# Whole numbers instead of a rounding operation in a piecewise-linear GELU

## The chip, the cores and the metric

The kernel runs on one core of a Trainium2 chip. The metric is the time of one execution on the device, in microseconds (us), smaller is better. Three runs of the kernel before gave 961.65, 962.42 and 962.64 us.

## The reference

Two transformer layers work on x (8 batches of 256 rows of 256). Each layer is a cross-attention on a context of the same shape and a feed-forward block, both behind a layernorm and with a residual. The feed-forward block of the first layer quantises to FP4. The change touches only the one of the second layer:

```python
def float2fix(x, mantissa_bits):
    s = jnp.float32(2.0 ** mantissa_bits)
    q = jnp.round(x * s) / s
    return x + stop_gradient(q - x)
def pwlin_gelu_basic(x, bits_in, bits_out):
    xq = float2fix(x, bits_in)
    y = jnp.interp(xq, _PWL_X, _PWL_Y)      # 33 knots on [-4, 4], 0.25 apart
    y = jnp.where(xq > 4.0, xq, jnp.where(xq < -4.0, 0.0, y))
    return float2fix(y, bits_out)
h = float2fix(x @ w1 + b1, 8)               # [.., 256] x [256, 1024]
h = float2fix(pwlin_gelu_basic(h, 8, 8), 8)
out = float2fix(h @ w2 + b2, 8)             # [.., 1024] x [1024, 256]
```

So the hidden value is rounded to a whole multiple of 2^-8, the exact GELU is taken at the two knots around it, and a straight line between them gives the result, rounded to 2^-8 again.

## The kernel before, in words

The 2048 rows are worked in four groups of 512. Every engine has its own program, written out by hand in the order in which it is to run; the engines meet only at semaphores. An opening does the first attention of group 0. For each group `fp4_and_layer1` does the FP4 block and the second attention. Between two groups stands a crossing: it does the last feed-forward block of the group that ends, and among it the first attention of the group that begins. There are three crossings, and a closing that does the last block of group 3 alone.

The block that the change touches is worked in eight chunks (m = 0 to 7) of 128 hidden columns by 512 rows. The path of one chunk goes through three engines, in one of four buffers of four slices (`gelu_buf`), with these lines of the profile:

- PE (`last_hidden`) multiplies by w1 into a PSUM bank, four banks in turn; in a crossing it then does the queries of the next group (`layer0_queries`, "ring,wq_s" in rows, tile q0 in banks 0 and 1).
- ACT L522 (`hidden`) evacuates the bank with the bias b1 into slice 0. ACT L527 (`hidden_fixed`) adds FIX = 1.5 x 2^15 to slice 0: fp32 then keeps whole multiples of 2^-8 only, and the last bits of the number are the whole number.
- DVE L838 keeps the bits above the lowest six (the knot, slice 2), DVE L843 keeps the lowest six (the place between the knots, slice 1).
- ACT L531 (`gelu_low`) is the GELU of the knot, ACT L535 (`gelu_high`) that of the knot 0.25 further; both take FIX off again by their bias. L535 waits until L531 is done.
- DVE L834 subtracts the two, L841 multiplies by the place between them, L847 adds the lower one, L849 rounds and writes `yT`. L841, L847 and L849 each wait until the one before is done. Where L849 is done, `y_ready` goes up.
- PE L1137 (`last_out`) multiplies by w2. In a crossing its order is: chunks 0 to 5, then the first scores of the next attention (`layer0_scores`, L1171), then chunks 6 and 7, then a product for the keys of the second attention (`layer1_key`), whose bank ACT empties at L548.

ACT and DVE interleave neighbouring chunks. ACT's order in one step is L522 of chunk m, L531 of m-1, L527 of m, L535 of m-1. DVE's is L834 of m-1, L838 of m, L841 of m-1, L843 of m, L847 and L849 of m-1. In a crossing ACT also puts the two query tiles into its last two steps (L542, two instructions for each, the second tile behind the last L535), and the first scores wait for both. Behind them stand a table load and the exponentials (L593), which wait for DVE's row maxima (L884).

Of the kernel before, what the change touches and what calls it, by code (L numbers as in the profile page):

```python
# [7 lines left out]
I32 = mybir.dt.int32  # L8
ALU = mybir.AluOpType
# [21 lines left out]
MASKED = -1.0e30  # L31
FIX = 1.5 * 2.0 ** 15
STEP = 0.25
KNOT_BITS, LINE_BITS = -64, 63
LINE_BASE = 2.0 ** 17
LINE_BASE_BITS = (127 + 17) << 23
# [175 lines left out]
def xattn_ffn_twice(nc, x, ctxT, mask, wq0, bq0, wk0, bk0, wv0, bv0, wo0, wgate, wup, wdown,  # L212
# [23 lines left out]
    with ExitStack() as ctx:  # L236
        def sb(name, shape, dt=F32):
            return ctx.enter_context(nc.sbuf_tensor(name, shape, dt))

        def sem(name):  # L240
            return ctx.enter_context(nc.semaphore(name))
# [15 lines left out]
        ident_s, ones_by_head = sb("ident_s", [P, P]), sb("ones_by_head", [P, 3, DK0])  # L257
        holder = sb("holder", [P, 1 + UNITS])
        minus_half = sb("minus_half", [P, TILES])
        gelu_bias, two, unused = sb("gelu_bias", [P, 3]), sb("two", [P, 1]), sb("unused", [P, 2])  # L260


        x_s, ctxT_s = sb("x_s", [P, TILES, DM]), sb("ctxT_s", [P, KC, GROUP])
# [57 lines left out]
        max0, inv0, clipped0 = sem("max0"), sem("inv0"), sem("clipped0")  # L321
        bias_ready, exp1, inv1, norm1 = (sem(n) for n in ("bias_ready", "exp1", "inv1", "norm1"))
        silu_ready, hid_ready = sem("silu_ready"), sem("hid_ready")
        g_fixed, g_knot, g_line, g_low, g_high, y_ready = (sem(n) for n in ("g_fixed", "g_knot", "g_line", "g_low", "g_high", "y_ready"))
        o_bias, o_round, out_ready = sem("o_bias"), sem("o_round"), sem("out_ready")

        def is_filled(at, key):
# [87 lines left out]
        @block.gpsimd  # L415
        def _(pool):
            for src, dst in ((bk0, bk0_s), (bq0, bq0_s)):
                for half in range(2):
                    pool.dma_start(dst[64 * half:64 * (half + 1), :], without_padding(src, half), allow_slow_non_contiguous=True).then_inc(keys_loaded, 16)
            pool.memset(minus_half[:], -0.5).then_inc(consts_set, 1)  # L420
            pool.memset(gelu_bias[:, 0:1], -FIX).then_inc(consts_set, 1)
            pool.memset(gelu_bias[:, 1:2], STEP - FIX).then_inc(consts_set, 1)
            pool.memset(v0[:], 0.0).then_inc(consts_set, 1)
            pool.memset(ones_by_head[:, 1, :], 0.0).then_inc(consts_set, 1)
            pool.memset(two[:], 2.0).then_inc(consts_set, 1)

            pool.memset(ones_by_head[:, 0:3:2, :], 1.0).then_inc(consts_set, 1)
            pool.memset(gelu_bias[:, 2:3], FIX).then_inc(consts_set, 1)
            pool.wait_ge(consts_set, 8)

            def ln_power(n):
                for h in range(HALVES):
                    half = slice(2 * h, 2 * h + 2)
                    pool.wait_ge(ln_var, n * HALVES + h + 1)
                    pool.tensor_tensor(rstd[:, half], var_eps[:, half], minus_half[:, half], ALU.pow).then_inc(ln_rstd, 1)  # L435

            def mask_to_bias():

                pool.tensor_scalar(maskbias[:], mask_s[:].bitcast(U8), MASKED, None, ALU.mult).then_inc(bias_ready, 1)

            def normalize_heads(g):

                for i in range(UNITS):
                    pool.wait_ge(inv1, g * UNITS + i + 1)
                    for a in range(2):
                        ins = pool.tensor_tensor(probs1[i % PRING1][:, a, :], probs1[i % PRING1][:, a, :],  # L446
                                                 row_inv[:, i, a:a + 1].to_broadcast([P, SEQ]), ALU.mult)
                    ins.then_inc(norm1, 1)

            def bias_x(g):  # L450

                pool.wait_ge(xn_ready, (0 if g == 0 else 4 * g - 1) * TILES + TILES)
                pool.tensor_tensor(x_s[:], x_s[:], bo0_s[:].unsqueeze(1).to_broadcast([P, TILES, DM]), ALU.add).then_inc(x_biased, 1)

            ln_power(0)
            pool.wait_ge(rest_loaded, 16 * 5)

            pool.wait_ge(max0, 1)
            bias_x(0)
            pool.wait_ge(mask_loaded, 16)  # L460
            pool.wait_ge(max0, 5)
            mask_to_bias()
            for g in range(GROUPS - 1):
                ln_power(g * 4 + 1)
                ln_power(g * 4 + 2)
                normalize_heads(g)
                pool.wait_ge(mask_loaded, g * 16 + 32)
                ln_power(g * 4 + 3)
                mask_to_bias()
                bias_x(g + 1)  # L470
                ln_power(g * 4 + 4)
            last = GROUPS - 1
            ln_power(last * 4 + 1)
            ln_power(last * 4 + 2)
            normalize_heads(last)
            ln_power(last * 4 + 3)

        @block.scalar
        def _(act):
# [38 lines left out]

            def hidden(at, m, buf):

                act.wait_ge(*is_filled(at, ("f", m)))
                act.activation(buf[:, 0, :], psum(at, ("f", m))[:], ACT.Identity, bias=b1_s[:, m:m + 1]).then_inc(drain(at, ("f", m)), 1)  # L522

            def hidden_fixed(at, g, m, buf):

                act.wait_ge(*is_drained(at, ("f", m)))
                act.activation(buf[:, 0, :], buf[:, 0, :], ACT.Identity, bias=gelu_bias[:, 2:3]).then_inc(g_fixed, 1)  # L527

            def gelu_low(g, m, buf):
                act.wait_ge(g_knot, g * (2 * FC1) + 2 * m + 1)  # L530
                act.activation(buf[:, 3, :], buf[:, 2, :], ACT.Gelu, bias=gelu_bias[:, 0:1]).then_inc(g_low, 1)  # L531

            def gelu_high(g, m, buf):
                act.wait_ge(g_low, g * FC1 + m + 1)
                act.activation(buf[:, 2, :], buf[:, 2, :], ACT.Gelu, bias=gelu_bias[:, 1:2]).then_inc(g_high, 1)  # L535

            def layer0_query(at, c):

# [11 lines left out]
            def last_layer(at, g, with_layer0):  # L550
# [5 lines left out]
                for m in range(FC1 + AHEAD):  # L556
# [4 lines left out]
                    u = m - AHEAD  # L561
                    if u >= 0:
                        gelu_low(g, u, gelu_buf[u % GELUS])
                    if m < FC1:
                        hidden_fixed(at, g, m, gelu_buf[m % GELUS])
                    if u >= 0:
                        gelu_high(g, u, gelu_buf[u % GELUS])
                    if with_layer0 and m >= FC1 + AHEAD - KEY_CHUNKS:
# [156 lines left out]
            for c in range(KEY_CHUNKS):  # L725
                layer0_query(opening_pass, c)
            piece_steps(1)
            act.wait_ge(consts_set, 8)
            layer0_heads(opening_pass, 0, True)
            act.wait_ge(rest_loaded, 16 * 5)  # L730
            for g in range(GROUPS - 1):
                fp4_and_layer1(middles[g], g)
                layer0_keys(crossings[g])
                last_layer(crossings[g], g, True)
                layer0_heads(crossings[g], g * UNITS + UNITS, False)
# [5 lines left out]
        def _(dve):  # L741
# [80 lines left out]
            def gelu(at, g):  # L822
# [6 lines left out]
                for m in range(FC1 + BEHIND):  # L829
# [4 lines left out]
                        dve.tensor_tensor(prev[:, 2, :], prev[:, 2, :], prev[:, 3, :], ALU.subtract).then_inc(g_line, 1)  # L834
                    if m < FC1:
                        buf = gelu_buf[m % GELUS]
                        dve.wait_ge(g_fixed, g * FC1 + m + 1)
                        dve.tensor_scalar(bits(buf[:, 2, :]), bits(buf[:, 0, :]), KNOT_BITS, None, ALU.bitwise_and).then_inc(g_knot, 1)  # L838
                    if u >= 0:
                        dve.wait_ge(g_line, line + 1)  # L840
# [208 lines left out]
            query_masks()  # L1049
            round_piece(0)  # L1050
            scale_piece(1)
            dve.wait_ge(consts_set, 7)
            layer0_heads(opening_pass, 0, None)
            dve.wait_ge(rest_loaded, 16 * 5)
            quantized_norm(opening_pass, 0)
# [15 lines left out]
        def _(pe):  # L1071
# [281 lines left out]
                    ins.then_inc(fill(at, key), 1)  # L1353


            pe.wait_ge(consts_set, 4)
            zeros = v0[:].rearrange("p t i n d -> p (t i n d)")
            for n in range(WARM_UP):
                pe.matmul(bank[7][:], zeros[:, 0:P], zeros[:, 0:512], start=True, stop=True)
# [89 lines left out]
```

## Time and profile before

| what | value |
| --- | --- |
| median of three runs | 962.42 us (961.65 to 962.64) |
| the profiled execution's own time | 961.48 us |
| its span | 959.6 us |
| PE / DVE / ACT / POOL busy | 94% / 70% / 64% / 21% of the span |
| granted TensorE clock, mean | 0.997 |

The span is the time from the first to the last instruction that the profiler saw; 1.9 us of the execution lie outside it. Busy shares are means over stages with different limits: a stage is read from its own rows. A row of a timeline gives start, time from there to the end of the last instruction of the row, engine, line, operation, output and input, and in brackets how long the engine had stood idle before and who ended that. The end of an instruction is its start and its duration; the next one of the same engine may start before it, since an engine overlaps neighbours that need nothing of each other.

### The profile page before, as it was taken

What the parts mean: (1) busy time and instruction counts of PE and PEld (TensorE: products, weight loads), DVE (VectorE), ACT (ScalarE), POOL (GpSimd) and SP (SyncE); (2) the same over time, 40 slices, a digit from 0 to 9 for tenths busy, and PEclk for the clock granted to TensorE, in tenths of its full rate; (3) what the DMA queues carried; (4) which work ended last, traced back from release to release, by engine and by line L of the source; (5) the groups of instructions that cost most, each with busy time, mean ns of one, the idle gap of its engine ahead of it and who ended that gap; (6) DMA issues with size and microseconds to landing.
All of it is one profiled execution on the core that took longest, in us unless ns stands there. A gap on an engine that the chain in (4) does not pass through costs nothing.

```text
span 959.6 us, 15982 instructions
## 1 busy us (share of the span) xinstructions
PE 902.0 (94%) x5514; PEld 587.4 (61%) x5514; DVE 674.2 (70%) x2153; ACT 615.8 (64%) x1681; POOL 198.3 (21%) x312
## 2 busy tenths in 40 slices
PE   6889999999999999999999999999999999999986
PEld 2555565767555565577665656567756556657744
DVE  4999882763889785474588879266488988647348
ACT  3788435972879643794578943498287964369544
POOL 3200001762000000475000000177300000047300
PEclk9999999999999999999999999999999999999999
DMA  9500100000000000000000010000000000000000
GB/s 296 192 1 2 28 0 23 2 1 1 1 1 24 3 26 23 1 2 1 0 1 13 12 28 1 23 1 2 1 0 2 17 8 1 0 1 2 1 1 22
DMA packets 14558, 18.32 MB, mean 19 GB/s; under 512 B 3088, under 2 KB 11664, under 8 KB 14480
## 3 DMA queue, kind: packets, MB, share of 16 engines
q1 hardware_dynamic: 12288, 15.40, 4.8%
q10 hardware_dynamic: 2064, 1.91, 0.7%
q8 instruction: 45, 0.74, 0.3%
q14 instruction: 33, 0.27, 0.1%
q0 software_dynamic: 128, 0.01, 0.0%
HBM read 15.21 MB, written 2.10 MB: 18 GB/s over the span
## 4 chain that ended last, share of the span: by engine, by line
PE 61%; DVE 22%; ACT 11%; issue 4%; POOL 1%; POOLq 0%; DVEq 0%
PE bank L1082 24%; PE bank L1097 9%; PE bank L1278 6%; PE bank L1258 5%; PE bank L1352 5%; PE bank L1194 4%; ACT ring L593 4%; DVE row_max L884 4%; PE bank L1171 2%; ACT ring L634 1%; PE bank L1210 1%; PE bank L1137 1%; ACT ring L517 1%; DVE ring L892 1%; PE bank L1324 1%
## 5 line engine op out<-in xcount | busy, mean ns | idle before, releaser
L435 POOL TENSOR_TENSOR rstd<-var_eps,minus_half 128x2 f32<-128x2 f32 x32 | 23.4, 735 | 589.2 <-DVE var_eps L798 589.2
L517 ACT ACTIVATE ring<-bank 128x512 f32<-128x512 f32 x224 | 123.4, 610 | 19.2 <-PE bank L1097 19.1
L446 POOL TENSOR_TENSOR ring<-ring,row_inv 128x256 f32<-128x256 f32 x192 | 112.1, 613 | 101.9 <-DVE row_inv L979 101.9
L1097 PE MATMUL bank<-ident_s,ring 128*128 128x128 f32 x768 | 105.3, 279 | 5.3 <-POOL ring L446 2.3
L1097 PEld LDWEIGHTS bank<-ident_s,ring 128*128 128x128 f32 x768 | 82.6, 141 | 40.2 <-issue 17.4
L634 ACT ACTIVATE ring<-ring,row_max 128x256 f32<-128x256 f32 x192 | 95.1, 497 | 17.3 <-DVE row_max L972 17.3
L593 ACT ACTIVATE ring<-bank,row_max 128x256 f32<-128x256 f32 x192 | 88.2, 492 | 4.7 <-DVE row_max L884 4.7
L972 DVE CUSTOM_DVE_ANT_0 ring<-bank,maskbias 128x256 f32<-128x256 f32 x192 | 70.7, 420 | 23.4 <-issue 23.4
L884 DVE TENSOR_REDUCE row_max<-bank 128x2 f32<-128x512 f32 x128 | 79.4, 683 | 5.9 <-PE bank L1171 5.1
L1082 PE MATMUL bank<-wgu_s,act_s 128*128 128x352 f32 x256 | 78.4, 459 | 0.0
L1082 PE MATMUL bank<-ctxT_s,wk_s 128*128 128x512 f32 x160 | 75.6, 596 | 0.7 <-DVE v L870 0.7
L1082 PE MATMUL bank<-wv_s,ctxT_s 128*128 128x512 f32 (+1 forms) x192 | 75.2, 524 | 0.0
L1258 PE MATMUL bank<-big_v,big_k 64*128 64x256 f32 x512 | 63.9, 388 | 2.0 <-DVE row_max L972 0.6
L1278 PE MATMUL bank<-ring,big_q 128*64 128x256 f32 x512 | 62.3, 385 | 1.6 <-ACT ring L517 1.6
L1082 PEld LDWEIGHTS bank<-wgu_s,act_s 128*128 128x128 f32 x256 | 47.7, 190 | 25.6 <-issue 1.9
L892 DVE TENSOR_SCALAR ring<-ring,row_inv 128x256 f32<-128x256 f32 x192 | 60.0, 356 | 3.4
L1137 PE MATMUL bank<-w_s,big_q 128*128 128x256 f32 x256 | 57.8, 382 | 3.3 <-DVE big_q L849 3.3
L1082 PE MATMUL bank<-act_s,wq_s 128*128 128x512 f32 x128 | 57.0, 598 | 3.1 <-issue 3.1
L1082 PE MATMUL bank<-act_s,w_s 128*128 128x512 f32 x128 | 57.5, 608 | 2.1 <-ACT ring L511 1.3
L1258 PEld LDWEIGHTS bank<-big_v,big_k 64*128 64x128 f32 x512 | 50.7, 186 | 14.2 <-issue 12.0
L1137 PEld LDWEIGHTS bank<-w_s,big_q 128*128 128x128 f32 x256 | 48.1, 190 | 13.8 <-DVE big_q L849 4.9
L1352 PE MATMUL bank<-wo_s,big_c 128*128 128x256 f32 x256 | 56.3, 381 | 0.0
(163 smaller groups left out, 1661.3 us busy)
## 6 DMA issues: line engine op xcount, KB each, us to landing
x_s<-x SPq DMA_DIRECT2D x4, 512.0 KB, 3.9
ctxT_s<-ctxT SPq DMA_DIRECT2D x4, 512.0 KB, 3.6
w_s<-w SPq DMA_DIRECT2D x2, 1024.0 KB, 16.4
out<-act_s SPq DMA_DIRECT2D x16, 128.0 KB, 1.7
wk_s<-wk SPq DMA_DIRECT2D x1, 1024.0 KB, 13.5
wv_s<-wv SPq DMA_DIRECT2D x1, 1024.0 KB, 14.8
wq_s<-wq SPq DMA_DIRECT2D x1, 1024.0 KB, 16.4
wo_s<-wo SPq DMA_DIRECT2D x1, 1024.0 KB, 16.6
```

The source lines that it names most:

```text
L446: ins = pool.tensor_tensor(probs1[i % PRING1][:, a, :], probs1[i % PRING1][:, a, :], row_inv[:, i, a:a + 1].to_broadcast([P, SEQ]), ALU.mult)
L517: act.activation(probsT[u % TRING][:, :, :].rearrange("p a q -> p (a q)"), psum(at, key)[:], ACT.Copy).then_inc(drain(at, key), 1)
L593: ins = act.activation(probs0[i % PRING0][:, a, :], psum(at, ("s0", i))[:, a * SEQ:(a + 1) * SEQ], ACT.Exp, bias=row_max[:, i, a:a + 1], a ...
L634: ins = act.activation(probs1[i % PRING1][:, a, :], probs1[i % PRING1][:, a, :], ACT.Exp, scale=-1.0, bias=row_max[:, i, a:a + 1], accum_o ...
L884: dve.tensor_reduce(row_max[:, i, :], psum(at, ("s0", i))[:].rearrange("p (a k) -> p a k", a=2), AX_X, ALU.max, negate=True).then_inc(max0, 1)
L972: ins = dve.tensor_tensor_reduce(probs1[i % PRING1][:, a, :], psum(at, ("s1", i))[:, a * SEQ:(a + 1) * SEQ], maskbias[:, 2 * b + a, :], -1 ...
L1082: ins = pe.matmul(dst, lhsT, rhs, start=(n == 0), stop=(n == len(pairs) - 1))
L1097: ins = pe.transpose(psum(at, key)[:, c * SEQ + a * P:c * SEQ + (a + 1) * P], tile[:, a, c * P:(c + 1) * P], ident_s[:])
L1137: ins = pe.matmul(psum(at, key)[:, n * DM:(n + 1) * DM], yT[:, m, t * P:(t + 1) * P], w2_s[:, m, :], start=(m == 0 and n == 0), stop=(m == ...
L1258: ins = pe.matmul(psum(at, key)[:, a * SEQ:(a + 1) * SEQ], q1[rows, p, b * SEQ + a * P:b * SEQ + (a + 1) * P], k1[rows, p, b * SEQ:(b + 1) ...
L1278: ins = pe.matmul(psum(at, key)[DK1 * j:DK1 * (j + 1), b * SEQ:(b + 1) * SEQ], v1[:, 2 * b + c, DK1 * head:DK1 * (head + 1)], probsT[u % T ...
L1352: ins = pe.matmul(psum(at, key)[:, 0:DM], c1[:, p, t * P:(t + 1) * P], wo1_s[:, p, :], start=(p == 0), stop=(p == PAIRS - 1))
```

## The change

ACT's evacuation writes int32 instead of fp32: it scales by 2^8 and adds the bias, which POOL has multiplied by 2^8 once. The number stored is then the whole number itself. `hidden_fixed` and its semaphore go. DVE's bit operations stay, and wait for the evacuation. The two GELUs read int32 and scale by 2^-8 at their input; the lower one has no bias any more, the upper one a bias of 0.25. POOL sets one constant instead of three, and multiplies the bias at the start.

```diff
-        gelu_bias, two, unused = sb("gelu_bias", [P, 3]), sb("two", [P, 1]), sb("unused", [P, 2])
+        gelu_bias, two, unused = sb("gelu_bias", [P, 1]), sb("two", [P, 1]), sb("unused", [P, 2])
...
             pool.memset(minus_half[:], -0.5).then_inc(consts_set, 1)
-            pool.memset(gelu_bias[:, 0:1], -FIX).then_inc(consts_set, 1)
-            pool.memset(gelu_bias[:, 1:2], STEP - FIX).then_inc(consts_set, 1)
+            pool.memset(gelu_bias[:], STEP).then_inc(consts_set, 1)
             pool.memset(v0[:], 0.0).then_inc(consts_set, 1)
...
             pool.memset(ones_by_head[:, 0:3:2, :], 1.0).then_inc(consts_set, 1)
-            pool.memset(gelu_bias[:, 2:3], FIX).then_inc(consts_set, 1)
-            pool.wait_ge(consts_set, 8)
+            pool.wait_ge(consts_set, 6)
...
             ln_power(0)
             pool.wait_ge(rest_loaded, 16 * 5)
+            pool.tensor_scalar(b1_s[:], b1_s[:], UNITS_OF_FIX, None, ALU.mult).then_inc(b1_scaled, 1)
...
             def hidden(at, m, buf):
                 act.wait_ge(*is_filled(at, ("f", m)))
-                act.activation(buf[:, 0, :], psum(at, ("f", m))[:], ACT.Identity, bias=b1_s[:, m:m + 1]).then_inc(drain(at, ("f", m)), 1)
-
-            def hidden_fixed(at, g, m, buf):
-
-                act.wait_ge(*is_drained(at, ("f", m)))
-                act.activation(buf[:, 0, :], buf[:, 0, :], ACT.Identity, bias=gelu_bias[:, 2:3]).then_inc(g_fixed, 1)
+                act.activation(buf[:, 0, :].bitcast(I32), psum(at, ("f", m))[:], ACT.Identity, bias=b1_s[:, m:m + 1],
+                               scale=UNITS_OF_FIX).then_inc(drain(at, ("f", m)), 1)
 
             def gelu_low(g, m, buf):
                 act.wait_ge(g_knot, g * (2 * FC1) + 2 * m + 1)
-                act.activation(buf[:, 3, :], buf[:, 2, :], ACT.Gelu, bias=gelu_bias[:, 0:1]).then_inc(g_low, 1)
+                act.activation(buf[:, 3, :], buf[:, 2, :].bitcast(I32), ACT.Gelu, scale=1.0 / UNITS_OF_FIX).then_inc(g_low, 1)
 
             def gelu_high(g, m, buf):
                 act.wait_ge(g_low, g * FC1 + m + 1)
-                act.activation(buf[:, 2, :], buf[:, 2, :], ACT.Gelu, bias=gelu_bias[:, 1:2]).then_inc(g_high, 1)
+                act.activation(buf[:, 2, :], buf[:, 2, :].bitcast(I32), ACT.Gelu, scale=1.0 / UNITS_OF_FIX, bias=gelu_bias[:, 0:1]).then_inc(g_high, 1)
...
-                    if m < FC1:
-                        hidden_fixed(at, g, m, gelu_buf[m % GELUS])
...
             act.wait_ge(rest_loaded, 16 * 5)
+            act.wait_ge(b1_scaled, 1)
...
-                        dve.wait_ge(g_fixed, g * FC1 + m + 1)
+                        dve.wait_ge(*is_drained(at, ("f", m)))
                         dve.tensor_scalar(bits(buf[:, 2, :]), bits(buf[:, 0, :]), KNOT_BITS, None, ALU.bitwise_and).then_inc(g_knot, 1)
...
-            pe.wait_ge(consts_set, 4)
+            pe.wait_ge(consts_set, 3)
```

ACT's order at the start of a crossing, before (the names are the buffers and banks of the first three chunks; in brackets the semaphores waited for):

```order
L522 ACTIVATE big_v<-bank,b_s 128x512 [waits filled0]
L527 ACTIVATE big_v<-big_v,gelu_bias 128x512 [waits drained0]
L522 ACTIVATE big_c<-bank,b_s 128x512 [waits filled1]
L531 ACTIVATE big_v<-big_v,gelu_bias 128x512 [waits g_knot]
L527 ACTIVATE big_c<-big_c,gelu_bias 128x512 [waits drained1]
L535 ACTIVATE big_v<-big_v,gelu_bias 128x512 [waits g_low]
L522 ACTIVATE big_c<-bank,b_s 128x512 [waits filled2]
L531 ACTIVATE big_c<-big_c,gelu_bias 128x512 [waits g_knot]
```

The same place now:

```order
L524 ACTIVATE big_v<-bank,b_s 128x512 [waits filled0]
L524 ACTIVATE big_c<-bank,b_s 128x512 [waits filled1]
L529 ACTIVATE big_v<-big_v 128x512 [waits g_knot]
L533 ACTIVATE big_v<-big_v,gelu_bias 128x512 [waits g_low]
L524 ACTIVATE big_c<-bank,b_s 128x512 [waits filled2]
L529 ACTIVATE big_c<-big_c 128x512 [waits g_knot]
```

One instruction of four has gone from each step, and the two GELUs of a chunk now stand directly behind each other. They keep the wait between them; the lower one (now L529) has lost its bias operand.

ACT's order at the end of a crossing, before (the last three GELU instructions, the queries, and the table load of the next attention):

```order
L535 ACTIVATE big_c<-big_c,gelu_bias 128x512 [waits g_low]
L542 ACTIVATE big_k<-bank,query_bias,query_scale 128x512 [waits filled0]
L542 ACTIVATE big_k<-bank,query_bias,query_scale 128x512
L531 ACTIVATE ring<-ring,gelu_bias 128x512 [waits g_knot]
L535 ACTIVATE ring<-ring,gelu_bias 128x512 [waits g_low]
L542 ACTIVATE big_k<-bank,query_bias,query_scale 128x512 [waits filled1]
L542 ACTIVATE big_k<-bank,query_bias,query_scale 128x512
L593 ACT_TABLE_LOAD
```

The same place now:

```order
L533 ACTIVATE big_c<-big_c,gelu_bias 128x512 [waits g_low]
L540 ACTIVATE big_k<-bank,query_bias,query_scale 128x512 [waits filled0]
L540 ACTIVATE big_k<-bank,query_bias,query_scale 128x512
L529 ACTIVATE ring<-ring 128x512 [waits g_knot]
L533 ACTIVATE ring<-ring,gelu_bias 128x512 [waits g_low]
L540 ACTIVATE big_k<-bank,query_bias,query_scale 128x512 [waits filled1]
L540 ACTIVATE big_k<-bank,query_bias,query_scale 128x512
L589 ACT_TABLE_LOAD
```

Nothing has moved here but the line numbers and the lower GELU's operand. The orders of DVE and PE are the same as before, instruction by instruction.

## Rows read from the trace of the kernel before

**Rows 1.** The page: busy time of PE, and the chain that ended last.
```profile
PE 902.0 (94%) x5514; PEld 587.4 (61%) x5514; DVE 674.2 (70%) x2153; ACT 615.8 (64%) x1681; POOL 198.3 (21%) x312
...
PE 61%; DVE 22%; ACT 11%; issue 4%; POOL 1%; POOLq 0%; DVEq 0%
```

**Rows 2.** The chain itself in the first crossing: start, us, what.
```profile
240.35 0.69 ACT big_c L522
...
242.90 0.69 DVE big_v L834
...
265.17 0.35 issue
```

**Rows 3.** Timeline of ACT, first crossing.
```profile
240.93 0.71 ACT L531 ACTIVATE big_v<-big_v,gelu_bias 128x512 f32<-128x512 f32 x1
241.54 0.71 ACT L527 ACTIVATE big_c<-big_c,gelu_bias 128x512 f32<-128x512 f32 x1
242.16 0.71 ACT L535 ACTIVATE big_v<-big_v,gelu_bias 128x512 f32<-128x512 f32 x1
...
243.96 0.72 ACT L531 ACTIVATE big_c<-big_c,gelu_bias 128x512 f32<-128x512 f32 x1 [0.52 <-DVE big_c L838]
...
262.35 0.72 ACT L531 ACTIVATE ring<-ring,gelu_bias 128x512 f32<-128x512 f32 x1
263.10 0.72 ACT L535 ACTIVATE ring<-ring,gelu_bias 128x512 f32<-128x512 f32 x1
263.73 1.43 ACT L542 ACTIVATE big_k<-bank,query_bias,query_scale 128x512 f32<-128x512 f32 x2
```

**Rows 4.** Timeline of DVE, first crossing.
```profile
243.51 0.42 DVE L838 TENSOR_SCALAR big_c<-big_c 128x512 int32<-128x512 int32 x1
...
245.50 0.43 DVE L849 TENSOR_SCALAR big_q<-big_v 128x512 f32<-128x512 f32 x1
245.94 0.69 DVE L834 TENSOR_TENSOR big_c<-big_c 128x512 f32<-128x512 f32 x1
...
261.16 0.69 DVE L834 TENSOR_TENSOR big_c<-big_c 128x512 f32<-128x512 f32 x1
...
263.76 0.43 DVE L849 TENSOR_SCALAR big_q<-big_c 128x512 f32<-128x512 f32 x1
264.11 0.68 DVE L834 TENSOR_TENSOR ring<-ring 128x512 f32<-128x512 f32 x1
...
266.27 0.43 DVE L849 TENSOR_SCALAR big_q<-ring 128x512 f32<-128x512 f32 x1
```

**Rows 5.** Timeline of PE, first crossing.
```profile
250.45 1.88 PE L1082 MATMUL bank<-ring,wq_s 128*128 128x512 f32 x4
252.62 1.98 PE L1082 MATMUL bank<-ring,wq_s 128*128 128x512 f32 x4 [0.29 <-ACT big_c L522]
254.44 10.52 PE L1137 MATMUL bank<-w_s,big_q 128*128 128x256 f32 x48
265.52 1.15 PE L1171 MATMUL bank<-big_k 32*128 32x256 f32 x16 [0.56 <-ACT big_k L542]
```

**Rows 6.** ACT groups by line and form: an operation without a bias operand.
```profile
L646 ACT ACTIVATE ring<-act_s 128x512 f32<-128x512 f32 x8 | 5.0, 630 | 10.7 <-DVE act_s L756 10.7
```

**Rows 7.** DVE L838, integer input and output, all instances: ns min/median/max.
```profile
L838 DVE TENSOR_SCALAR big_c<-big_c x16: 418/420/422, 243.5 to 944.2; 128x512 int32<-128x512 int32 x16
```

**Rows 8.** POOL L439, integer input, all instances: the same columns.
```profile
L439 POOL TENSOR_SCALAR maskbias<-mask_s x4: 2776/2776/2777, 36.0 to 673.9; 128x1024 f32<-128x1024 uint8 x4
```

**Rows 9.** Timeline of POOL, opening.
```profile
5.30 0.11 POOL L421 MEMSET gelu_bias<- 128x1 f32 x1
...
26.20 2.37 POOL L453 TENSOR_TENSOR x_s<-x_s,bo_s 128x1024 f32<-128x1024 f32 x1 [16.48 <-DVE row_max L884]
```

**Rows 10.** Timelines of DVE and PE, closing.
```profile
928.38 0.69 DVE L834 TENSOR_TENSOR big_v<-big_v 128x512 f32<-128x512 f32 x1 [2.03 <-ACT big_v L535]
...
952.23 1.99 PE L1137 MATMUL bank<-w_s,big_q 128*128 128x256 f32 x8 [0.52 <-DVE big_q L849]
```

More of the change, by code:

```diff
@@ L33 @@
 STEP = 0.25
+UNITS_OF_FIX = 2.0 ** 8
 KNOT_BITS, LINE_BITS = -64, 63
@@ L323, in xattn_ffn_twice @@
         silu_ready, hid_ready = sem("silu_ready"), sem("hid_ready")
-        g_fixed, g_knot, g_line, g_low, g_high, y_ready = (sem(n) for n in ("g_fixed", "g_knot", "g_line", "g_low", "g_high", "y_ready"))
+        g_knot, g_line, g_low, g_high, y_ready = (sem(n) for n in ("g_knot", "g_line", "g_low", "g_high", "y_ready"))
+        b1_scaled = sem("b1_scaled")
         o_bias, o_round, out_ready = sem("o_bias"), sem("o_round"), sem("out_ready")
@@ L727, in _ @@
             piece_steps(1)
-            act.wait_ge(consts_set, 8)
+            act.wait_ge(consts_set, 6)
             layer0_heads(opening_pass, 0, True)
             act.wait_ge(rest_loaded, 16 * 5)
+            act.wait_ge(b1_scaled, 1)
             for g in range(GROUPS - 1):
@@ L1051, in _ @@
             scale_piece(1)
-            dve.wait_ge(consts_set, 7)
+            dve.wait_ge(consts_set, 6)
             layer0_heads(opening_pass, 0, None)
```

## The prediction

> **What bounds the kernel now.** I read the page first, for the shares and the chain that ended last; then the chain inside one crossing; then the timelines of ACT, DVE and PE there, since the chain names only the last of several waits; then the same place in the closing. The page says little here: PE is busy for 94% of the span, the chain is PE's for 61%, DVE's for 22%, ACT's for 11% [rows 1]. The instruction that goes is ACT's (L527), 32 of them at 0.71 us. Their sum, 22.7 us, is not what can be won: ACT overlaps neighbours and waits anyway.
>
> In a crossing the chain goes through ACT from 240.35, through DVE from 242.90, and ends with the queries, 0.35 us of issue and the first scores [rows 2]. So there are three limits to follow.
>
> ACT and DVE as a loop: DVE's L834 starts at 242.90 and at 245.94, a step of 3.04 us [rows 2, 4]. Inside it stand L834 to L838, 0.61; L838 to ACT's L531, 0.45; L531 to L527, 0.61; L527 to L535, 0.62; and L535 with its hand-over, 0.74. These make 3.03 [rows 2 to 4]. ACT sits idle for 0.52 us before L531 at 243.96 [rows 3], so it is not full; the loop is closed by the two waiting for each other.
>
> DVE by itself: where ACT has long finished, at the last chunk, L834 follows L849 after 0.35 us (263.76 to 264.11); in the loop it takes 0.44 (245.50 to 245.94). From 261.16 to 264.11 the step is 2.95 us [rows 4]. That is what DVE needs alone.
>
> PE: chunks 0 to 5 of L1137 stand in one row of 48 instructions with no idle inside, up to 264.96. PE's only waits here are 0.29 us before the second query product (for L522 of chunk 5, whose bank it takes) and 0.56 before the scores, for the queries [rows 5]. PE is thus nearly the bound of the crossing, and what these two gaps hold is the most that ACT can give back.
>
> **The change part by part.**
>
> *The first step.* ACT's L522 at 240.35 still waits for PE. L531 follows at 240.93, L527 at 241.54, L535 at 242.16, DVE at 242.90 [rows 2, 3]. L527 leaves, but its 0.61 us are not won whole: L535 waits for L531, and such a pair is 0.75 us apart where nothing stands between (262.35 to 263.10), against 1.23 now, so 0.48 is won [rows 3]. The lower GELU also loses its bias operand. ACT's 512-wide instruction without one takes 0.630 us [rows 6], those with one 0.71 to 0.72 [rows 3], so 0.08 more. First L834: 0.48 + 0.08 = 0.56 earlier, 242.34. Without the 0.08 it is 0.48.
>
> The Trainium skill, page "ScalarE: Activation LUTs", section "What ACT_TABLE_LOAD costs", gives about 93 ns for a pointer operand and says that back-to-back ACTIVATEs overlap by about 93 ns. The trace has 0.08 and 0.10; by the page the first step would win 0.57. The overlap speaks against the naive sum: it is lost between two instructions of which one waits for the other.
>
> *The steps behind it.* The loop without L527 is 0.61 + 0.45 + 0.67 (the pair, with the shorter lower GELU) + 0.74 = 2.47 us, which is under DVE's 2.95 [rows 3, 4]. So DVE sets the step. It wins 3.04 - 2.95 = 0.09 us in each of six steps (the seventh is at 2.95 already), 0.56. DVE's last L834, L849 and y_ready come 0.56 + 0.56 = 1.12 us earlier.
>
> *The closing.* There DVE's chain ends the kernel: its first L834 waits 2.03 us for ACT as in a crossing, and PE waits 0.52 us for the last L849 [rows 10]. Everything behind moves along. Won: 1.12.
>
> *A crossing.* The last L838 stands 0.61 behind the L834 of chunk 6, which moves from 261.16 to 260.04. L838 ends at 261.07, the last L531 starts at 261.11 (now 262.35, behind a query), L535 at 261.78, the second query pair at 262.41 instead of 263.73: 1.32 earlier [rows 3, 4]. PE may not be able to use that. Its streams start at fixed distances: the query product's four instructions at 250.45 need 1.72 us until the next could start, 252.17, and the gap makes it 252.62; the row's four take 1.82 to 254.44, of which 0.10 is the pipe filled anew. That gap costs 0.55. The 48 instructions of L1137 are (10.52 - 0.38) / 47 = 0.216 us apart, so the scores could start at 254.44 + 10.36 = 264.80 and start at 265.52: 0.72 (0.38 is one instruction of the group) [rows 5]. Together 1.27: the scores start at 264.25. The queries are ready at 265.17 - 1.32 = 263.85, or 264.20 with the 0.35 of issue [rows 2]. Just in time. Chunk 7 of L1137 comes to PE about 2.8 us behind the start of the scores (their 1.15 less an overlap, and eight times 0.216), at 267.0; its y is ready at 266.70 - 1.12 = 265.58 [rows 4]. So 1.26 us in each of three crossings, 3.78. Reading only the idle in brackets (0.29 + 0.56 = 0.85) would give 2.55 for the three.
>
> On this the Trainium skill, page "TensorE: Matmul & The Clock Gate", section "Step-by-step: what each phase is for", says that one matmul's drain overlaps the fill of the next, so that a stream costs its columns alone. By that rule, the trace agrees: one instruction lasts 0.38 us, and they come 0.216 apart. By the bracketed idle a crossing would win 0.85, by the streams 1.26.
>
> *The rest.* POOL has one small constant fewer ahead of PE's first work; it is worth at most its 0.11 us [rows 9], I take 0.04. The new multiplication of 128x8 on POOL stands ahead of L453, where POOL waits 16.48 us for DVE until 26.20 [rows 9]. That wait hides it, if the bias has landed; even at the 2.37 us of L453 it delays nothing that PE needs before the first attention is done. ACT's added wait for it comes long after. Queued behind it are ACT's steps of the FP4 block.
>
> *What no row shows* is ACT reading or writing int32. Below nothing: one element is one element, no reason for a gain. At no cost: DVE's int32 instruction takes 0.420 us, its fp32 one (L849) 0.43 [rows 4, 7]. Above: POOL's one-input instruction on integers takes 2.776 us, a two-input one in fp32 of the same size 2.37 [rows 8, 9], 17% more. On ACT that is 0.11 for each of three instructions. Then the first step wins 0.56 - 0.33 = 0.23, the closing 0.79, a crossing 0.77 (the queries decide), and the sum is 0.79 + 2.31 = 3.1. I take nothing, since 512 int32 elements are as many bytes and as many elements, and DVE's row is the nearest in shape.
>
> **Sum:** 1.12 + 3.78 + 0.04 = 4.9 us. The profiled execution took 961.48, so 956.5. It was 0.94 under the median of 962.42; from the median the sum gives 957.5. Own range: 3.1 (integers at 17%) to 5.1 (POOL's whole 0.11, a little from table and exponentials) off, 957.3 to 959.3, with about half a us for the runs.
>
> **The rivals.**
>
> *PE is no limit.* If all 1.32 of the queries and more passed, a crossing would give 1.4 and the sum 5.3: 957.1. Against: PE's streams have only 1.27 in them. It lies within my range, 5%.
>
> *The crossings give it back.* Behind the scores stand DVE's row maxima, which follow the last L849 and so come only 1.12 earlier, the table load, the exponentials, and ACT's L548. If one of these or the order among them keeps the old time, only the closing's 1.12 is left: 961.3; if half is kept, 959.4. For: PE, ACT and DVE hand over to each other within tenths there. Against: the chain has no outside event in it, no DMA, and everything in the chain moves by at least 1.1. Chance 11%, most of it at the lower gain.
>
> *ACT is slow with integers: slower than before.* Price d for each of L522, L531, L535. The first step changes by -0.56 + 3d, and from d = 0.24 on the loop (2.47 + 2d) is longer than DVE's 2.95 and sets the step. All is used up at about d = 0.27, 43% of the 0.63 us. At half speed d is 0.43: first step 0.73 later, steps of 3.33 instead of 3.04, six of them 1.7 later, the closing 2.5 us and a crossing about 3 us later: 962.4 + 2.5 + 9 = 974. For: no row shows it. Against: rows 7, and the 17% of POOL stays far below 43%. Chance 6%.
>
> *It does not do what it says:* the lower GELU keeps a pointer bias. Then the pair stays 0.75 apart; the closing gives 1.04, a crossing 1.16, the sum 4.6: 957.9. Inside my own case.
>
> **How the numbers follow.** My case, with the last rival in it, 73%; PE no limit 5%; given back 11%; slow integers 6%; 5% for what I don't see, of either sign. Predicted 957.5. The range 956.7 to 960.0 holds my case with half a us of spread, the first rival, and a half-kept gain. A measurement can tell about 0.2%, 1.9 us, from no change. Faster by more than that: 0.73 + 0.05 + about half of the given-back case 0.05 = 0.83. Same: 0.10. Slower: 0.07.
>
> **What would show it.** In a crossing: L834 steps of 2.95 us with no wait for ACT behind the first; ACT's idle before the lower GELU longer, about 1 us; the second query product with no idle before it; the scores starting 23.9 us behind the L522 of chunk 1 instead of 25.17 (240.35 to 265.52), with an idle below 0.1 before them. The lower GELU at 0.63, the upper at 0.71, the evacuation at 0.67. Wrong would be: any of these above 0.8, L834 still waiting for ACT, or the first scores at their old distance.

## The result and the profile after

The changed kernel took 956.53 us (median of 5 runs, 956.17 to 956.94), the kernel before 961.89 in the same comparison (5 runs, 961.65 to 962.64): ratio 0.9943, 95% interval 0.9928 to 0.9957, 5.4 us less. A second comparison gave 956.71 against 961.48: 0.9950, 0.9937 to 0.9962, 4.8 us less. The direction was forecast, and the size nearly: 957.5 was predicted, and 956.53 lies 0.17 us below the range.

The profiled execution took 956.21 us, with a span of 954.4. Its page, busy times and chain:

```profile
PE 900.4 (94%) x5514; PEld 588.9 (62%) x5514; DVE 672.2 (70%) x2153; ACT 596.3 (62%) x1649; POOL 198.7 (21%) x311
...
PE 68%; DVE 18%; ACT 9%; issue 4%; POOL 1%; POOLq 0%; DVEq 0%
```

Beside [rows 1]: ACT has 19.5 us less to do, the span is 5.2 us shorter, and the chain has moved from DVE and ACT to PE. ACT in the first crossing (start, time, line, operation, idle before and who ended it; L524 is the evacuation, L529 and L533 are the two GELUs):

```profile
241.53 0.69 ACT L524 ACTIVATE big_c<-bank,b_s 128x512 int32<-128x512 f32 x1 [1.03 <-PE bank L1079]
242.11 0.62 ACT L529 ACTIVATE big_v<-big_v 128x512 f32<-128x512 int32 x1
242.76 0.72 ACT L533 ACTIVATE big_v<-big_v,gelu_bias 128x512 f32<-128x512 int32 x1
...
247.52 0.63 ACT L529 ACTIVATE big_c<-big_c 128x512 f32<-128x512 int32 x1 [0.98 <-DVE big_c L835]
```

Integers cost ACT nothing: 0.69 for the first evacuation as before, 0.63 and 0.72 for the GELUs. L533 follows 0.65 us behind L529, and from the third chunk on ACT stands idle for 0.98 us before each lower GELU, where [rows 3] had 0.52. DVE in the same crossing (L831 and L846 are the old L834 and L849):

```profile
243.52 0.69 DVE L831 TENSOR_TENSOR big_v<-big_v 128x512 f32<-128x512 f32 x1 [2.23 <-ACT big_v L533]
...
246.12 0.43 DVE L846 TENSOR_SCALAR big_q<-big_v 128x512 f32<-128x512 f32 x1
246.46 0.68 DVE L831 TENSOR_TENSOR big_c<-big_c 128x512 f32<-128x512 f32 x1
```

L831 comes 0.34 us behind L846 instead of 0.44, and the step is 2.94 us where [rows 4] had 3.04: DVE no longer waits for ACT behind its first step. The first L831 stands 1.99 us behind the second evacuation's start, [rows 2] had 2.55: 0.56 earlier, as worked out. PE there:

```profile
237.82 13.97 PE L1079 MATMUL bank<-act_s,w_s 128*128 128x512 f32 x32 [0.45 <-ACT ring L512]
251.63 3.60 PE L1079 MATMUL bank<-ring,wq_s 128*128 128x512 f32 x8
255.06 10.52 PE L1134 MATMUL bank<-w_s,big_q 128*128 128x256 f32 x48
265.51 1.15 PE L1168 MATMUL bank<-big_k 32*128 32x256 f32 x16
```

Both gaps of [rows 5] are gone. From the first w1 product to the first scores it is 27.69 us, where it was 28.88 (236.64 to 265.52): 1.19. The other crossings are alike. Their w1 products start at 237.82, 465.56, 693.32, and the closing's at 918.08; before these were 236.64, 465.58, 694.52 and 920.49. So the three stretches between them are shorter by 1.20, 1.18 and 1.21 us, 3.59 together.

What is left is in the opening and in the closing, and there the granted clock has a part that I had not reckoned with. Windows of PE before (from and to; length, busy time and instructions, granted clock, share of the DMA engines, GB/s):

```profile
24.00:28.00 4.00, 3.84 (x29) 1.00 1.03 399
...
918.00:922.00 4.00, 2.16 (x6) 0.79 0.02 4
922.00:926.00 4.00, 4.00 (x8) 0.78 0.00 0
```

And after:

```profile
24.00:28.00 4.00, 4.00 (x24) 0.64 1.02 394
...
916.00:920.00 4.00, 2.58 (x9) 1.00 0.02 6
920.00:924.00 4.00, 4.00 (x11) 1.00 0.00 0
```

Before, the clock was below its upper level of 2.4 GHz at the start of the closing, whose w1 products took 15.59 us; after, it was at it, and they took 13.97. In the opening it is the other way round: the changed kernel's clock fell while PE did the products for the values of the first attention. The same row before and after:

```profile
25.24 3.72 PE L1082 MATMUL bank<-wv_s,ctxT_s 128*128 128x256 f32 x16
```
```profile
24.75 5.41 PE L1079 MATMUL bank<-wv_s,ctxT_s 128*128 128x256 f32 x16
```

It took 1.69 us more, although it started 0.49 earlier, since PE's first eight products, which are there only to warm it up, took 6.01 us instead of 6.46. The first crossing then starts 1.18 us later than before. The account of the two profiled executions is, in us after less before:

| stretch | difference |
| --- | --- |
| opening, PE's start and the warm-up products | -0.49 |
| opening, values product (clock) | +1.69 |
| opening, the rest | -0.02 |
| three crossings with the blocks between them | -3.59 |
| closing, w1 products (clock) | -1.62 |
| closing, the rest | -1.17 |
| sum | -5.20 |

The change gives 4.76 of it in crossings and closing, and 0.03 by PE's earlier start (6.78 us instead of 6.81). The two falls of the clock, one in each execution, nearly cancel. What is left over is the warm-up, 0.46, which the experiments had to explain.

### The profile page after: what moved, and what is told of

It is laid out like the page before. It is cut to its first block, busy times and chain, and to the rows that moved or that the text cites. A ratio compares the mean times of both kernels' runs of the same rounds, so it can differ in the third digit from the quotient of the medians.

```text
span 954.4 us, 15949 instructions
## 1 busy us (share of the span) xinstructions
PE 900.4 (94%) x5514; PEld 588.9 (62%) x5514; DVE 672.2 (70%) x2153; ACT 596.3 (62%) x1649; POOL 198.7 (21%) x311
## 4 chain that ended last, share of the span: by engine, by line
PE 68%; DVE 18%; ACT 9%; issue 4%; POOL 1%; POOLq 0%; DVEq 0%
PE bank L1079 28%; PE bank L1094 9%; PE bank L1275 6%; PE bank L1255 5%; PE bank L1349 5%; PE bank L1134 5%; PE bank L1191 4%; ACT ring L589 4%; DVE row_max L881 4%; PE bank L1168 2%; ACT ring L630 2%; ACT ring L518 1%; PE bank L1207 1%; DVE ring L889 1%; PE bank L1321 1%
```

## The experiments

Every kernel was compared with the kernel before on the same chip; rounds with 13 to 20 runs of it had medians of 961.48 to 961.71.

**The changed kernel again.** No edit.

> The changed kernel once more. Theory (stream and clock): in the first profile of the change, three crossings gave 3.6 us and the closing 1.17 us; beside that the granted clock fell in the opening (a loss of 1.2 us) and did not fall in the closing (a gain of 1.6 us). If that is the accident of one execution, another profile shows another pattern, and the runs spread over about 1.5 us. If it belongs to the instruction times of this kernel, the pattern is there again: 0.68 at 26 to 30 us, 1.00 at 918 us, span 954.4. Median 956.5 either way.

956.71 us. The opening was at full clock this time and the closing was not. Its w1 products, in a timeline of PE:

```profile
236.67 13.97 PE L1079 MATMUL bank<-act_s,w_s 128*128 128x512 f32 x32 [0.45 <-ACT ring L512]
...
916.88 15.67 PE L1079 MATMUL bank<-act_s,w_s 128*128 128x512 f32 x32 [0.73 <-issue]
```

So one program has the fall in the opening in one execution and that in the closing in another. The spread, 0.9 us, was smaller than I had said. The two profiles differ by 1.15 us in the opening and 1.70 in the closing, with opposite signs. The 1.15 is again a difference of two things: the values product took 3.72 us here, 1.69 less, and the warm-up row 6.54 instead of 6.01.

**An operation put back on ACT, for nobody.**

```diff
+                    if m < FC1:
+                        act.wait_ge(filled_in, g * FC1 + m)
+                        act.activation(filler[:, 1, :], filler[:, 0, :], ACT.Identity, bias=gelu_bias[:, 0:1]).then_inc(filled_in, 1)
                     if u >= 0:
                         gelu_high(g, u, gelu_buf[u % GELUS])
```

> The changed kernel with a 128x512 operation with a bias put back on ACT where hidden_fixed stood, on a tile of its own, for which nobody waits; DVE still waits for the evacuation alone. Theory (DVE sets the step): the pair of GELUs is 1.15 us apart, the loop 2.94 us and so still at DVE's 2.94; only the first step is later, by 0.48. Closing +0.48; in a crossing the queries come 0.48 later, of which 0.2 is slack at PE: +0.28 each. In sum +1.3 us, 957.8. Rival (what L527 cost on ACT is what was won): nearly all comes back, 961.2.

959.69, but in two groups: four of ten runs at 955.9 to 957.2, six at 959.6 to 960.2, with granted clocks of 0.998 and 0.999 against 0.995 and 0.996. Its profiled execution, one of the six (959.88), has both falls: 5.41 us for the values product, 15.61 for the closing's w1 products. The median says nothing by itself; I ran it again with the clock held (below).

**Queries earlier on ACT.**

```diff
-                    if with_layer0 and m >= FC1 + AHEAD - KEY_CHUNKS:
-                        layer0_query(at, m - (FC1 + AHEAD - KEY_CHUNKS))
+                    if with_layer0 and FC1 - KEY_CHUNKS <= m < FC1:
+                        layer0_query(at, m - (FC1 - KEY_CHUNKS))
```

> The changed kernel with the two query tiles on ACT one step earlier, behind the upper GELUs of chunks 5 and 6 instead of 6 and 7. Theory (PE's stream bounds the crossing): the scores already follow PE's stream without a gap, so queries that are ready 2 to 3 us sooner bring nothing; DVE's last steps come up to 0.7 us later, which has slack: 956.5, plus 0 to 1 us. Rival (the queries still bound the crossing): three crossings win up to 1 us or more each, 953.5 or less.

956.23 us (four runs, 955.93 to 958.86): no different from the changed kernel. The profiled execution is the one of 958.86, and it too has both falls (5.41 and 16.17); the crossings lie outside them, at a granted clock of 1.00. ACT and PE in its first crossing:

```profile
260.87 1.43 ACT L540 ACTIVATE big_k<-bank,query_bias,query_scale 128x512 f32<-128x512 f32 x2
```
```profile
251.70 3.60 PE L1079 MATMUL bank<-ring,wq_s 128*128 128x512 f32 x8
255.13 10.52 PE L1134 MATMUL bank<-w_s,big_q 128*128 128x256 f32 x48
265.59 1.15 PE L1168 MATMUL bank<-big_k 32*128 32x256 f32 x16
```

The queries are ready at 262.30, 3.3 us ahead of the scores, and these still start 13.89 us behind the query product, against 13.88 (251.63 to 265.51). PE's stream bounds the crossing, and the rival is refuted.

**The kernel before without hidden_fixed, in fp32.** It leaves out the rounding of the hidden value.

```diff
-                    if m < FC1:
-                        hidden_fixed(at, g, m, gelu_buf[m % GELUS])
...
-                        dve.wait_ge(g_fixed, g * FC1 + m + 1)
+                        dve.wait_ge(*is_drained(at, ("f", m)))
```

> The kernel before without hidden_fixed, all in fp32; leaves out the rounding of the hidden value, so that the bits mean something else. Theory (integers on ACT cost nothing): first step 0.48 earlier and not 0.56, for the lower GELU keeps its bias; DVE's step 2.94. Closing -1.1, crossings -1.2 each (PE's stream bounds them): 957.2 if the clock in opening and closing stays as in the kernel before, 956.8 if it changes as in the changed one. Rival (the integer forms cost or save something): over 0.5 us away from the changed kernel at the same clock pattern, and ACT durations that differ from 0.67, 0.72 and 0.72 us.

956.66 us (955.93 to 957.02), the time of the changed kernel. ACT's groups (line, names, shapes, count; busy us, mean ns; idle before):

```profile
L531 ACT ACTIVATE big_c<-big_c,gelu_bias 128x512 f32<-128x512 f32 x16 | 11.6, 722 | 12.6 <-DVE big_c L836 12.6
L535 ACT ACTIVATE big_c<-big_c,gelu_bias 128x512 f32<-128x512 f32 x16 | 11.6, 722 | 0.5
```

And all instances of the same place in the changed kernel (ns min/median/max), with integers:

```profile
L529 ACT ACTIVATE big_c<-big_c x16: 629/630/632, 244.6 to 939.5; 128x512 f32<-128x512 int32 x16
...
L533 ACT ACTIVATE big_c<-big_c,gelu_bias x16: 722/722/724, 245.2 to 940.2; 128x512 f32<-128x512 int32 x16
...
L524 ACT ACTIVATE big_c<-bank,b_s x16: 667/669/687, 241.5 to 934.9; 128x512 int32<-128x512 f32 x16
```

A GELU with a bias takes 722 ns on fp32 and on int32. The integers are what allows L527 to go; by themselves they neither cost nor save.

**The clock's falls taken away.** PE gets products of no use in its gaps of the opening (behind the first queries) and of the closing (between the two halves' transposes). Four kernels: both kernels with both, the changed one with the opening's alone, the one before with the closing's alone.

```diff
             layer0_queries(opening_pass)
+            pe.matmul(bank[7][:], zeros[:, 0:P], zeros[:, 0:512], start=True, stop=True)
+            pe.matmul(bank[7][:, 0:256], zeros[:, 0:P], zeros[:, 0:256], start=True, stop=True)
...
                 for h in range(HALVES):
+                    if not with_layer0 and h == 1:
+                        wait_free(at, ("f", 0))
+                        for n in range(2):
+                            pe.matmul(bank[0][:], ident_s[:], w1_s[:, 0, 0:512], start=True, stop=True)
                     pe.wait_ge(xn_ready, ln * TILES + 2 * h + 2)
```

> The kernel before with two products of no use (512 and 256 wide) in PE's 1.8 us gap of the opening and two (512 wide) in its 2.6 us gap of the closing, so that PE does not stand idle there. Theory (the clock falls there by accident, in some executions and not in others): granted clock 1.00 from 20 to 34 us and through the closing's w1 products, which take 14.0 us instead of 15.6. 959.9 to 960.1 and a narrower spread. Rival (the clock has nothing to do with PE's idle there): 961.5, clock low as before.

> The changed kernel with the same products of no use. Theory: clock 1.00 in opening and closing; it stands 3 x 1.20 + 1.17 = 4.8 us under the kernel before with the same products, in every execution: 955.1 to 955.3. Rival (the change itself gives 5.3 us and the clock is no part of it): the difference between the two filled kernels is 5.3 or more.

> The changed kernel with the products of no use in the opening alone. Theory: no low clock at 24 to 30 us, PE's first values product takes 3.7 us and not 5.4; the closing stays an accident, so two levels 1.6 us apart: 955.2 and 956.8. Rival: opening still low in one of several executions, levels 1.2 us apart.

> The kernel before with the products of no use in the closing alone. Theory: w1 products of the closing in 14.0 us instead of 15.6, so 1.6 us less than the kernel before where the opening has the same clock: 959.9; 1.2 us more where the opening is slow. Rival (the closing's clock was no loss): 961.5.

| kernel | before | changed |
| --- | --- | --- |
| with both | 959.67 (959.20 to 960.06) | 954.31 (953.92 to 954.91) |
| opening's alone | | 956.88 (955.86 to 956.98) |
| closing's alone | 960.28 (958.64 to 961.11) | |

The clock did what was expected in all four profiles; the times did so less well. With both, 959.9 to 960.1 and 955.1 to 955.3 were expected, and both kernels came out lower. With one alone the runs fall into groups (955.86 against 956.86 to 956.98; 958.6 to 958.8, 959.6 to 959.8 and 960.7 to 961.1), not at the distances expected. The changed kernel with both, closing, as a window and in the timeline of PE:

```profile
905.00:934.00 29.00, 27.42 (x95) 1.00 0.00 1
```
```profile
914.39 0.66 PE L1087 MATMUL bank<-ident_s,act_s 128*128 128x128 f32 x4 [0.85 <-DVE act_s L800]
915.78 13.97 PE L1079 MATMUL bank<-act_s,w_s 128*128 128x512 f32 x32 [0.73 <-issue]
```

With the opening's alone the closing's w1 products took 15.67 us again. All 17 profiles together: with products of no use in the opening the values product took 3.72 us in ten of ten; without them it took 5.41 in three of seven, the three whose warm-up row was shortest (5.90 to 6.08 us, against 6.40 to 6.54 in the other four). With products of no use in the closing its w1 products took 13.97 us in ten of ten; without them 15.59 to 16.17 in six of seven. The one without the fall is the first profile of the changed kernel. So PE's idle in these two places is what lets the clock fall. Filling both is worth 1.8 us to the kernel before (0.9979 of it, 0.9970 to 0.9989) and 2.2 to 2.4 to the changed one.

The two filled kernels, however, stand 5.36 apart and not 4.8, and that is the number that the rival had named. Their profiled executions are 6.03 apart. The stretches between the w1 products and the closing give 4.71 of it; 1.29 lies ahead of the first w1 product, nearly all of it in the eight warm-up products: they took 6.71 us in one and 5.47 in the other. Within such a row the longest product lasts 1.22 us and the shortest 0.59. I read that as the clock rising among them; the profile doesn't show it, since the granted clock stands at 1.00 there from the start.

**The pair again, and two parts of the change on it.** The same edits; the third kernel has the ACT operation from above as well, the fourth a bias operand of 0 at the lower GELU (`bias=gelu_bias[:, 1:2]`).

> The kernel before with the products of no use in opening and closing, once more, to measure the change on one chip with the clock's falls taken away. Theory: 959.6, spread under 1 us; what spread is left comes from the warm-up products, whose clock rises at another point in each execution (5.5 to 6.7 us for the eight).

> The changed kernel with the same products, once more. Theory: by the rows 3 x 1.18 + 1.18 = 4.7 us under before_filled_b; the 5.36 of the first pair held 0.6 us of luck in the warm-up, so 954.9 now if that is luck. Rival (something in the opening is faster for good in the changed kernel): 5.3 us apart again, with the first key product earlier by 0.5 us or more.

> The changed kernel with the products of no use and the 128x512 operation on ACT in the place of hidden_fixed, for which nobody waits. Theory (DVE sets the step; only the first step and the second query product are later): by its first profile 3 x 0.45 + 0.55 = 1.9 us over the filled changed kernel, 956.5. Rival (the whole of the change is ACT's time): 4.7 us over it, 959.3.

> The changed kernel with the products of no use and a pointer bias of 0 at the lower GELU. Theory: that instruction 0.72 instead of 0.63, the pair 0.75 apart; DVE's step stays 2.94; closing 0.08 later; in a crossing the queries come 0.16 later, within the 0.2 of slack before PE: scores unmoved. 0.1 us over the filled changed kernel. Rival (queries bound the crossing): scores 0.16 later each, 0.6 us in sum.

959.30 (958.67 to 960.14) and 954.27 (953.98 to 954.82): 5.03 apart, between the 4.7 of the theory and the 5.3 of the rival. By the profiles crossings and closing give 4.78, and the first key product came 0.89 earlier (12.46 against 13.35), which is what the rival had asked for (0.5 or more).

The kernel with the ACT operation took 956.69 (955.90 to 956.84), 2.4 over the filled changed kernel and 2.6 under the filled one before; 1.9 was expected. By its profile the three stretches are 0.45 longer each than in after_filled_b and the closing 0.55 (36.90 against 36.35), which is 1.9; its warm-up took 0.4 longer. ACT and DVE in its first crossing:

```profile
240.66 0.62 ACT L530 ACTIVATE big_v<-big_v 128x512 f32<-128x512 int32 x1
241.17 0.71 ACT L565 ACTIVATE filler<-filler,gelu_bias 128x512 f32<-128x512 f32 x1
241.79 0.71 ACT L534 ACTIVATE big_v<-big_v,gelu_bias 128x512 f32<-128x512 int32 x1
```
```profile
242.53 0.69 DVE L836 TENSOR_TENSOR big_v<-big_v 128x512 f32<-128x512 f32 x1 [2.69 <-ACT big_v L534]
...
245.48 0.69 DVE L836 TENSOR_TENSOR big_c<-big_c 128x512 f32<-128x512 f32 x1
```

All of ACT's time is back, and DVE's step is 2.95 us and not 3.04. What came back is the first step (the pair is 1.13 us apart instead of 0.65) and a part of PE's gaps, as the theory has it. The other 2.9 of the 4.8 us stay won although ACT has as much to do as before: here DVE still takes the evacuation's result directly and doesn't wait for an operation between. No run puts that wait back alone. The crossings lose 0.45 and not the 0.28 I had said at first: before the scores PE has 0.18 us of idle, and the second query product starts a little later again.

The kernel with the bias operand took 954.31 (953.75 to 955.25), no different from the one without. ACT and PE, first crossing:

```profile
240.57 0.71 ACT L530 ACTIVATE big_v<-big_v,gelu_bias 128x512 f32<-128x512 int32 x1
241.31 0.72 ACT L534 ACTIVATE big_v<-big_v,gelu_bias 128x512 f32<-128x512 int32 x1
```
```profile
263.97 1.15 PE L1173 MATMUL bank<-big_k 32*128 32x256 f32 x16
```

The pair is 0.74 apart instead of 0.65, and the scores are where they were: 27.70 us behind the w1 product (236.27). The bias operand costs something in the closing alone, 0.06 us (36.41 against 36.35).

**Where PE starts.** Two filled kernels with one constant more or fewer ahead of PE's first product, and the filled changed kernel beside them.

```diff
 (changed kernel)
             pool.memset(gelu_bias[:], STEP).then_inc(consts_set, 1)
+            pool.memset(unused[:, 0:1], 0.0)
             pool.memset(v0[:], 0.0).then_inc(consts_set, 1)
 (kernel before; pe waits for 3 constants instead of 4)
-            pool.memset(gelu_bias[:, 0:1], -FIX).then_inc(consts_set, 1)
...
             pool.memset(two[:], 2.0).then_inc(consts_set, 1)
+            pool.memset(gelu_bias[:, 0:1], -FIX).then_inc(consts_set, 1)
```

> The changed kernel with the products of no use, and one constant more set on POOL ahead of the clearing of v0, so that PE's first product starts at 6.82 as in the kernel before and not at 6.78. Theory (what is over the 4.7 us of crossings and closing is luck in the warm-up's clock): 954.3 as without it, warm-up row anywhere between 5.5 and 6.7 us. Rival (PE's start decides where the clock rises): warm-up 6.4 to 6.7, first key product at 13.1 or later, 954.8.

> The kernel before with the products of no use, one constant set behind the clearing of v0 instead of ahead, so that PE starts at 6.78. Theory (luck): 959.5 as without it, row anywhere. Rival (the start decides): warm-up 5.5 to 6.2, first key product at 12.8 or earlier, 959.0.

> The changed kernel with the products of no use for the third time, beside the two others on one chip: 954.3; its distance to constant_back_filled is the price of the later start, 0.04 us by the theory, 0.5 by the rival.

954.02 (953.56 to 955.11), 959.56 (958.46 to 960.08) and 954.65 (953.57 to 955.06). The constant decides nothing: with it the changed kernel was not slower, and without it the kernel before was not faster. The one profile with the constant put back has the long warm-up that the rival asked for, but it is of the slowest of five executions (955.11; the others took 953.56 to 954.64). Warm-up rows of three kernels, with PE starting at 6.78 and with it at 6.81 or 6.82 (after_both_filled, constant_back_filled, before_filled_b):

```profile
6.78 5.47 PE L1360 MATMUL bank<-v 128*128 128x512 f32 x8 [6.78 <-POOL two L426]
```
```profile
6.81 6.66 PE L1361 MATMUL bank<-v 128*128 128x512 f32 x8 [6.81 <-POOL two L427]
```
```profile
6.82 6.68 PE L1363 MATMUL bank<-v 128*128 128x512 f32 x8 [6.82 <-POOL two L425]
```

Over all 17 profiles the row lasts from 5.47 to 6.75 us. The last two of these are of a changed kernel and of one before with nearly the same warm-up: their spans are 953.3 and 958.2, 4.9 us apart.

## Why the prediction was right or wrong

*The mechanism held.* ACT and DVE as a loop of 3.04 us, DVE by itself at 2.95, PE's two gaps as the most that a crossing can give back: each was seen, and queries_early, act_filler_filled and low_bias_filled tell them apart from the rivals. The first step came 0.56 earlier, as worked out, the step was 2.94 against 2.95.

*The terms.* A crossing was forecast at 1.26 and gave 1.19 to 1.21: the gap before the scores was worth 0.63 (11.08 us from the first L1137 to the scores before, 10.45 after) and not 0.72, since the step from the last w2 product to the first scores is 0.31 us (10.45 less 47 steps of 0.216), and I had counted it as one more step of 0.216. Reading the idle in brackets alone (0.85) would have been further off. The closing was forecast at 1.12 and gave 1.17. Sum 4.9 forecast, 4.76 in the rows, and 4.9 between two executions with nearly the same warm-up.

*Integers* cost nothing, the value I took; the 17% that widened the range upwards did not come.

*What failed is the last step, from the sum to the time and its range.* The sum was made against the profiled execution's 961.48, and gave 956.5, where 956.53 was measured. I then put it on the median of three runs, 962.42, for 957.5, and let the range go only 0.8 below that. That median was high: 15, 20, 13 and 15 further runs have their medians at 961.48 to 961.71. Of the 0.97 us between 957.5 and the measured 956.53 the base thus makes 0.7 to 0.9; on the right base the range would have begun near 956. That 956.5 is met so closely is partly luck: the sum was 0.2 over the rows' 4.76, and the changed kernel's shorter warm-up gave something more, 0.46 in the profiled execution. The range's low edge also allowed nothing for the clock beyond half a us for the runs. The sign was in the trace of before, in its chain of waits (start, us, what), for the same eight instructions of w1 products in a crossing and in the closing:

```profile
236.64 3.69 PE bank L1082 x8
...
920.49 5.30 PE bank L1082 x8
```

Whether PE's clock falls in the opening (1.7 us) and in the closing (1.6 us or more) differs between executions of one program, and so does the length of the warm-up (up to 1.3 us). The sum had no term for any of the three.

*The rivals.* PE is no limit: refuted by queries_early. The crossings give it back: refuted, 1.20 comes through each to the next block. Slow integers: refuted. The lower GELU keeps its bias: it did not, and it would have cost 0.1 and not the 0.3 of my sum, since the queries have slack before PE.

*Open.* The medians of the three filled kernels with the old evacuation have a mean of 959.5, those of the four with the changed one 954.3: 5.2 apart, against 4.7 to 4.9 by the rows. The place of the difference is the warm-up row: its mean is 6.51 us over the six profiles with the old evacuation and 6.12 over the eleven with the new one, and in each of the three filled pairs it is the changed kernel's that is shorter. The two sets overlap (6.32 to 6.71 and 5.47 to 6.75), and the constant ahead of PE's start is not the reason. Whether the 0.3 to 0.5 us is luck or something steady was not settled.

*A faster version.* The changed kernel with the products of no use takes 954.3 to 954.7 us, 0.9925 (0.9911 to 0.9938) of the kernel before, and beats both.

## What to carry to other kernels

An instruction taken out of one engine is worth what the loop it stands in loses before the next engine becomes the bound: here 22.7 us of ACT's work gave 4.8. Find the second bound (the distance of the same instructions where nobody waits) and the third (the gaps in PE's stream, counted from start to start, since each holds more than the idle shown) before making the sum. And make sum and range on the same base: the profiled execution's own time, with what the clock can add or take, by rows of such a fall, in any stretch where PE stands idle.

## What the runs showed of the hardware

ACT reads and writes int32 at the speed of fp32: 630 ns for 128x512 without a bias operand, 722 with one (722 in fp32 too), 669 for an evacuation (672 in fp32). PE's granted clock can fall behind gaps of 1.8 us (opening) and of 2.6 and 0.7 us (closing) in one execution of a program and not in the next: without anything in them it fell in three of seven profiles (opening) and in six of seven (closing), at a price of 1.7 and 1.6 to 2.2 us. With a few products of no use in them it stayed at 2.4 GHz in ten of ten, for each of the two places. One kernel (act_filler) had runs in two groups, 955.9 to 957.2 and 959.6 to 960.2; those of the first have the higher mean clock.
